# Layer 0's attention one chunk earlier, its router logits as extra columns of the key and value products, and the attention output as the opening term of the experts' sum

## The reference, cut to what matters

```python
xn = layernorm(x)
# attention: 16 heads of 8, linear attention with rope
q, k, v = split(xn @ W_qkv);  q, k = rope(q), rope(k)
qf, kf = elu(q * 8**-0.5) + 1, elu(k) + 1
out = (qf @ (kf.T @ v)) / max(qf @ kf.sum(0), 1e-6)     # per sequence and head
att = out @ W_out
# feed-forward: 64 experts of width 64, top 8 of 4 of 8 groups, and one shared expert
scores = sigmoid(xn @ router_w.T)                        # the logits are 64 columns a token
coef   = 2.5 * normalised top-8 scores (bias added for the choice only)
moe    = sum_e coef[:, e] * ((silu(xn @ Wg[e]) * (xn @ Wu[e])) @ Wd[e])
shared = (silu(xn @ SWg) * (xn @ SWu)) @ SWd
x = x + att + moe + shared
```

## Time and profile before

| | us |
|---|---|
| median of 3 executions | 1829.75 (1829.34 to 1831.74) |
| profiled execution, its own time | 1833.56 |
| its span in the trace | 1831.3 |
| PE busy | 1736.6 (95%) |
| DVE busy | 1348.7 (74%) |
| ACT busy | 803.2 (44%) |
| POOL busy | 609.8 (33%) |
| longest idle of PE in its own rows, chunks 1 to 14 | 0.4 |

### The profile page before, as it was taken

How to read it: one execution, slowest core, us unless ns; L and a number is a source line. 1 busy time by engine, 2 the same in 40 slices (tenths; PEclk the granted TensorE clock), 3 DMA queues, 4 the chain that set the end, 5 groups by cost and what they waited for, 6 DMA issues and landing times.

```text
span 1831.3 us, 25191 instructions
## 1 busy us (share of the span) xinstructions
PE 1736.6 (95%) x7292; PEld 1225.3 (67%) x7292; DVE 1348.7 (74%) x4012; ACT 803.2 (44%) x1439; POOL 609.8 (33%) x637
## 2 busy tenths in 40 slices
PE   3999999999999999999999999999999989888885
PEld 2667777777777777777767677777777766565653
DVE  5667878787878787878787878787878864553447
ACT  4435353535353535353535353535353434432321
POOL 6212142423232323232323232323231333565550
PEclk9999999999999999999999999999999999999988
DMA  7948464636464636463636363636454444666559
GB/s 213 257 125 238 97 157 101 157 95 163 97 161 97 160 97 160 97 161 94 161 96 163 90 167 94 160 95 162 101 148 102 111 143 141 187 204 213 173 158 298
DMA packets 166470, 269.80 MB, mean 147 GB/s; under 512 B 13688, under 2 KB 52344, under 8 KB 166080
## 3 DMA queue, kind: packets, MB, share of 16 engines
q1 hardware_dynamic: 157760, 250.50, 51.9%
q0 software_dynamic: 8576, 17.70, 3.0%
HBM read 202.21 MB, written 65.93 MB: 146 GB/s over the span
## 4 chain that ended last, share of the span: by engine, by line
PE 88%; another core or an unknown queue 3%; issue 3%; ACT 2%; DMA 2%; DVE 2%; POOL 1%; SPq 0%; ACTq 0%; DVEq 0%; POOLq 0%
PE ps_y L656 24%; PE ps_gate L603 8%; PE ps_gate L602 8%; PE ps_gate L601 7%; PE ps_up L601 7%; PE ps_up L603 7%; PE ps_up L602 7%; PE ps_y L682 3%; PE ps_side L622 2%; PE ps_side L601 2%; PE ps_side L603 2%; PE ps_side L602 2%; PE ps_side L791 1%; PE ps_side L774 1%
## 5 line engine op out<-in xcount | busy, mean ns | idle before, releaser
L854 DVE TENSOR_TENSOR silu_h<-ps_up,silu_h 128x512 f32<-128x512 f32 x618 | 424.4, 687 | 401.9 <-ACT silu_h L1260 260.5
L1260 ACT ACTIVATE silu_h<-ps_gate 128x512 f32<-128x512 f32 x618 | 368.0, 599 | 614.1 <-PE ps_gate L603 535.6
L656 PE MATMUL ps_y<-silu_h,w_dn 128*128 128x512 f32 x1056 | 540.6, 593 | 0.4 <-ACT yT L1266 0.4
L848 DVE TENSOR_TENSOR silu_h<-coef_b,silu_h 128x512 f32<-128x512 f32 x528 | 373.9, 708 | 9.0 <-DMA coef_b<-coef_kept 6.6
L601 PE MATMUL ps_gate<-xnT,w_gu 128*128 128x512 f32 x528 | 318.4, 603 | 0.0
L656 PEld LDWEIGHTS ps_y<-silu_h,w_dn 128*128 128x128 f32 x1056 | 199.4, 189 | 55.0 <-issue 7.7
L601 PE MATMUL ps_up<-xnT,w_gu 128*128 128x512 f32 x528 | 210.3, 398 | 11.0 <-DVE silu_h L854 6.6
L602 PE MATMUL ps_gate<-xnT,w_gu 128*128 128x512 f32 x528 | 211.2, 400 | 0.0
L602 PE MATMUL ps_up<-xnT,w_gu 128*128 128x512 f32 x528 | 209.7, 397 | 0.0
L603 PE MATMUL ps_up<-xnT,w_gu 128*128 128x512 f32 x528 | 209.1, 396 | 0.0
L603 PE MATMUL ps_gate<-xnT,w_gu 128*128 128x512 f32 x528 | 207.4, 393 | 0.0
(11 more groups left out here) (265 smaller groups left out, 2719.9 us busy)
## 6 DMA issues: line engine op xcount, KB each, us to landing
coef_b<-coef_kept SPq DMA_DIRECT2D x256, 512.0 KB
slots_x<-empty SPq DMA_DIRECT2D x15, 2080.0 KB, 12.3
w_block<-w_kept SPq DMA_DIRECT2D x45, 512.0 KB
xs<-slots_x SPq DMA_DIRECT2D x37, 260.0 KB
y_back<-y_kept SPq DMA_DIRECT2D x15, 512.0 KB, 7.1
w_raw<-in_ffn_w SPq DMA_DIRECT2D x49, 128.0 KB, 4.1
w_down<-in_ffn_w SPq DMA_DIRECT2D x45, 128.0 KB
xres<-in_x SPq DMA_DIRECT2D x16, 256.0 KB, 3.1
```

The source lines that it names most:

```text
L656: eng.matmul(ps_y[:, :], w_dn[:, j], silu_h[:, g % HBUFS], start=j == 0, stop=last).then_inc(pe_down)
L848: eng.tensor_tensor(silu_h[:, s], coef_b[:, q % COEF_RING, k], silu_h[:, s], ALU.mult).then_inc(dve_h)
L854: eng.tensor_tensor(silu_h[:, s], ps_up[g % 2][:, :], silu_h[:, s], ALU.mult).then_inc(dve_h1)
L1260: eng.activation(silu_h[:, s], ps_gate[g % 2][:, :], ACT.Silu).then_inc(act_silu)
```

## The change

`ATTENTION0` moves to other tiles (6 to 29) and is run for chunk c + 1 in chunk c, after `ROUTE0` in the list; chunk 15 has none of it. In chunk 0 its own attention runs as before (`EARLY0`), and that of chunk 1 by a table of its own (`SECOND0`). `logit0` is gone from chunk 2 on: the router's weights lie beside the value weights, `kv0` to `kv3` are 320 columns wide, ACT copies 192 instead of 128 columns to `v0`, and `score_exp`, now at tile 11, reads the logits there. The product with `w_out` opens the sum in `ps_y` at tile 0 (in chunk 0 it comes at tile 15). The sends of `ROUTE1` are due at tiles 4 to 12 instead of 10 to 21; its `softmax` is at 19 instead of 23, `gate_exp` at 15 instead of 12; `ATTENTION1` is mostly one tile later. `feat_exp` is at 15, `k_feat` 17, `kvsum` 19, `kvmask` 20, `num0` 21.

```diff
-ATTENTION0 = [(0, "kv0"), (1, "kv1"), (2, "kv2"), (3, "kv3"), (4, "k_rope"), (5, "q"), (6, "q_cos"), (6, "q_swap"), (7, "q_sin"), (8, "q_min"),
-              (12, "feat_exp"), (13, "q_feat"), (14, "k_feat"), (16, "kvsum"), (17, "kvmask"), (19, "num0"), (20, "num1"), (20, "mix0"),
-              (24, "mix1"), (26, "mixT")]
+ATTENTION0 = [(6, "kv0"), (7, "kv1"), (8, "kv2"), (9, "kv3"), (10, "k_rope"), (11, "q"), (12, "q_cos"), (12, "q_swap"), (14, "q_sin"), (14, "q_min"),
+              (15, "feat_exp"), (16, "q_feat"), (17, "k_feat"), (19, "kvsum"), (20, "kvmask"), (21, "num0"), (22, "num1"), (23, "mix0"),
+              (24, "mix1"), (29, "mixT")]
...
-ROUTE0 = [(0, "stats0"), (2, "norm0"), (4, "xT0"), (5, "x_lo0"), (8, "logit0"), (10, "score_exp"), (12, "sigmoid0"), (14, "sigmoid1"),
+ROUTE0 = [(0, "stats0"), (2, "norm0"), (4, "xT0"), (5, "x_lo0"), (11, "score_exp"), (13, "sigmoid0"), (15, "sigmoid1"),
           (18, "choice"), (18, "pair4"), (19, "pair2"), (20, "pair1"), (21, "gtop"), (22, "gstrike"), (23, "groups"), (24, "top8"),
           (25, "strike"), (26, "weigh"), (28, "coefT")]
-ROUTE1 = [(5, "stats1"), (7, "norm1"), (8, "xT1"), (9, "x_lo1"), (10, "vl0"), (10, "vl1"), (11, "top1"), (12, "gate_exp"), (23, "softmax"), (30, "select"),
-          (31, "prefix"), (39, "rank"), (40, "key"), (41, "first2"), (42, "slot"), (43, "send0"), (45, "send1"), (47, "send2"), (48, "send3"),
-          (49, "send4"), (51, "send5"), (53, "send6"), (54, "send7")]
+ROUTE1 = [(5, "stats1"), (7, "norm1"), (8, "xT1"), (9, "x_lo1"), (10, "vl0"), (10, "vl1"), (11, "top1"), (15, "gate_exp"), (19, "softmax"), (30, "select"),
+          (31, "prefix"), (33, "rank"), (34, "key"), (35, "first2"), (36, "slot"), (37, "send0"), (38, "send1"), (39, "send2"), (40, "send3"),
+          (42, "send4"), (43, "send5"), (44, "send6"), (45, "send7")]
...
-ATTENTION1 = [(10, "q1"), (11, "v1"), (12, "s0"), (13, "s0_mask"), (13, "s1"), (14, "s1_mask"), (15, "top"), (16, "strike0"), (17, "strike1"),
-              (18, "attend_exp"), (21, "sum0"), (22, "sum1"), (23, "p0"), (23, "near"), (24, "p1"), (24, "self"), (25, "add1"), (26, "hear1"), (26, "mixa"),
...
+ATTENTION1 = [(10, "q1"), (11, "v1"), (13, "s0"), (14, "s0_mask"), (14, "s1"), (15, "s1_mask"), (16, "top"), (17, "strike0"), (18, "strike1"),
+              (19, "attend_exp"), (22, "sum0"), (23, "sum1"), (24, "p0"), (24, "near"), (25, "p1"), (25, "self"), (26, "add1"), (27, "hear1"), (27, "mixa"),
...
-        steps += [(ATTENTION0 if c > 0 else EARLY0, c)]
-        steps += [(ROUTE0, c + 1)] if c + 1 < CHUNKS else []
+        if c == 0:
+            steps += [(EARLY0, 0), (SECOND0, 1), (ROUTE0_SECOND, 1)]
+        elif c + 1 < CHUNKS:
+            steps += [(ROUTE0, c + 1), (ATTENTION0, c + 1)]
...
-                if last:
+                if j == 0 and c > 0:
+                    eng.wait_ge(act_y, c)
+                if j == (0 if c > 0 else FIRST_MIX):
                     eng.wait_ge(*read("mixT", c))
                     eng.wait_ge(w_out_in, 16)
-                    eng.matmul(ps_y[:, :], w_out[:, :], mix_a[:, :], start=False, stop=False).then_inc(pe_mix)
+                    eng.matmul(ps_y[:, :], w_out[:, :], mix_a[:, :], start=j == 0, stop=False).then_inc(pe_mix)
...
-                    mm3(ps[:, 0:2 * P], row(halves(key), int(what[2])), w0_part(2 * P, 4 * P)).then_inc(signal)
+                    mm3(ps[:, 0:2 * P + EXPERTS0], row(halves(key), int(what[2])), w0_part(2 * P, 4 * P + EXPERTS0)).then_inc(signal)
...
+                        for r in range(ROWS):
+                            eng.wait_ge(*read(f"kv{r}", c))
+                        eng.activation(score0[:, :].rearrange("p (r e) -> p r e", r=ROWS), v0[:, :, 0:EXPERTS0], ACT.Exp, scale=-1.0).then_inc(act_score)
...
-                    eng.copy(v0[:, r, 0:P], side_bank(what, c)[:, P:2 * P]).then_inc(read(what, c)[0])
+                    eng.copy(v0[:, r, 0:EXPERTS0 + P], side_bank(what, c)[:, P:2 * P + EXPERTS0]).then_inc(read(what, c)[0])
```

More of the change, by code:

```diff
@@ L85 @@
                 (30, "gates"), (33, "gatesT")]
-ATTENTION1 = [(10, "q1"), (11, "v1"), (12, "s0"), (13, "s0_mask"), (13, "s1"), (14, "s1_mask"), (15, "top"), (16, "strike0"), (17, "strike1"),
-              (18, "attend_exp"), (21, "sum0"), (22, "sum1"), (23, "p0"), (23, "near"), (24, "p1"), (24, "self"), (25, "add1"), (26, "hear1"), (26, "mixa"),
-              (26, "add2"), (27, "hear2"), (27, "mixa_add"), (27, "add3"), (28, "hear3"), (28, "add4"), (29, "hear4"), (32, "mixl"), (32, "mixl_add")]
-ATTENTION1_UNITS = [(at if what == "v1" else at + 2, what) for at, what in ATTENTION1]
+ATTENTION1 = [(10, "q1"), (11, "v1"), (13, "s0"), (14, "s0_mask"), (14, "s1"), (15, "s1_mask"), (16, "top"), (17, "strike0"), (18, "strike1"),
+              (19, "attend_exp"), (22, "sum0"), (23, "sum1"), (24, "p0"), (24, "near"), (25, "p1"), (25, "self"), (26, "add1"), (27, "hear1"), (27, "mixa"),
+              (27, "add2"), (28, "hear2"), (28, "mixa_add"), (28, "add3"), (29, "hear3"), (29, "add4"), (30, "hear4"), (32, "mixl"), (32, "mixl_add")]
+ATTENTION1_UNITS = [(at if what == "v1" else at + (2 if what == "q1" else 1), what) for at, what in ATTENTION1]
 PREP1 = [(28, "w1"), (29, "fold"), (30, "fold_lo"), (31, "zero")]
@@ L99 @@
 EARLY0 = [(1, "feat_exp"), (3, "q_feat"), (4, "k_feat"), (6, "kvsum"), (7, "kvmask"), (8, "num0"), (9, "num1"), (9, "mix0"), (10, "mix1"), (12, "mixT")]
+SECOND0 = [(13, "kv0"), (14, "kv1"), (15, "kv2"), (16, "kv3"), (17, "k_rope"), (17, "q"), (18, "q_cos"), (20, "q_swap"), (21, "q_sin"), (22, "q_min"),
+           (23, "feat_exp"), (24, "q_feat"), (25, "k_feat"), (26, "kvsum"), (27, "kvmask"), (28, "num0"), (29, "num1"), (29, "mix0"), (30, "mix1"), (31, "mixT")]
+ROUTE0_SECOND = [(8, "logit0")] + [(at - (what == "score_exp"), what) for at, what in ROUTE0]
+FIRST_MIX = 15
 TAKES = {"xT0": "x_lo0", "logit0": "score_exp", "coefT": "coefT", "kv0": "kv0", "kv1": "kv1", "kv2": "kv2", "kv3": "kv3",
@@ L209, in build_program @@
         mix_rows = tmp0
-        v0 = sb("v0", [ROWS, P + 1])
+        v0 = sb("v0", [ROWS, EXPERTS0 + P + 1])
         kv = sb("kv", [SEQS, P + HEADS])
@@ L332, in build_program @@
             sem(n) for n in ("dve_kparts", "pool_krope", "pool_kmin", "pool_qrope", "pool_qmin"))
-        act_kexp, act_qexp, act_qrelu, dve_kfeat, pool_qfeat = (
-            sem(n) for n in ("act_kexp", "act_qexp", "act_qrelu", "dve_kfeat", "pool_qfeat"))
+        act_score, act_kexp, act_qexp, act_qrelu, dve_kfeat, pool_qfeat = (
+            sem(n) for n in ("act_score", "act_kexp", "act_qexp", "act_qrelu", "dve_kfeat", "pool_qfeat"))
         dve_gate, act_gate, dve_sel, dve_slot, dve_gw, dve_gates, pool_mark, pool_before, dve_logit1, dve_strike1, act_attend, dve_sum, act_keys = (
@@ L653, in last_products @@
                     eng.wait_ge(w_dn_in[j // DOWN_PART], 16)
-                if j == 0 and c > 0:
-                    eng.wait_ge(act_y, c)
-                eng.matmul(ps_y[:, :], w_dn[:, j], silu_h[:, g % HBUFS], start=j == 0, stop=last).then_inc(pe_down)
+                eng.matmul(ps_y[:, :], w_dn[:, j], silu_h[:, g % HBUFS], start=g == 0, stop=last).then_inc(pe_down)
             def first_of_unit(u):
@@ L700, in step @@
                     for r in range(ROWS):
-                        ins = mm3(ps[:, r * EXPERTS0:(r + 1) * EXPERTS0], row(halves(key), r), w0_part(4 * P, 4 * P + EXPERTS0))
+                        ins = mm3(ps[:, r * EXPERTS0:(r + 1) * EXPERTS0], row(halves(key), r), w0_part(3 * P, 3 * P + EXPERTS0))
                     ins.then_inc(signal)
@@ L724, in step @@
                         for r in (2 * s, 2 * s + 1):
-                            ins = eng.matmul(ps[:, s * (P + 1):(s + 1) * (P + 1)], kf[:, r * P:(r + 1) * P], v0[:, r],
+                            ins = eng.matmul(ps[:, s * (P + 1):(s + 1) * (P + 1)], kf[:, r * P:(r + 1) * P], v0[:, r, EXPERTS0:],
                                              start=r == 2 * s, stop=r == 2 * s + 1)
@@ L883, in step @@
                 elif what == "sigmoid0":
-                    eng.wait_ge(*read("logit0", c))
+                    if c <= 1:
+                        eng.wait_ge(*read("logit0", c))
+                    else:
+                        eng.wait_ge(act_score, c - 1)
                     keep(eng.tensor_scalar(score0[:, :], score0[:, :], 1.0, None, ALU.add))
@@ L1235, in vector @@
             eng.memset(gsel[:, :, :], 0.0)
-            eng.memset(v0[:, :, P:], 1.0).then_inc(dve_const)
+            eng.memset(v0[:, :, EXPERTS0 + P:], 1.0).then_inc(dve_const)
             for n, (what, key) in enumerate(prologue):
@@ L1321, in step @@
                 elif what == "score_exp":
-                    eng.wait_ge(*done("logit0", c))
                     if c > 0:
                         eng.wait_ge(coef_rows, c)
-                    eng.activation(score0[:, :], side_bank("logit0", c)[:, 0:ROWS * EXPERTS0], ACT.Exp, scale=-1.0).then_inc(read("logit0", c)[0])
+                    if c <= 1:
```

(8 more changed lines are left out.)

## The result

The changed kernel takes **1859.68 us** (median of 4, 1858.87 to 1860.74); the kernel before, run beside it, 1830.74 (4 runs). The ratio on record for the runs is 1.0145, interval 1.0127 to 1.0163; the two medians alone give 1.0158, inside it. The kernel is slower, by far more than the 0.2% that a measurement of this kernel can tell. The forecast was 1852, with a range of 1808 to 1862. The profiled execution took 1860.74 for a span of 1858.5, which is 27.2 over the span before.

What follows compares the result with a forecast made beforehand. The prediction took TensorE's (PE's) own queue to bound the steady chunks. From a median of 1829.75: -13.6 PE's work, -7 chunk 15, +32 `num0` waits, +11.5 clock give 1852.7, forecast 1852, range 1808 to 1862.

Steps and rivals of the forecast that it cites:

- likeliest case: PE waits at `num0` for a late `kvmask` in chunks 1 to 14, half followed by clock falls: 1852, chance 0.5.
- the last rival: In chunk 15 DVE's `first2` still waits because a send is late elsewhere: 7 more than the forecast, 1859; chance 0.03.
- PE's work: Logit products removed less 64 added columns: net 1.00 for each of chunks 2 to 15, less 0.34 for chunk 1: -13.6.
- `num0` waits: In chunks 1 to 14 PE waits 2.3 at `num0`, tile 21, for DVE's `kvmask`: +32.
- clock: Half of the 14 waits at `num0` are followed by a lower PE clock, 1.65 each: +11.5.
- chunk 15: DVE's first wait for sends goes; 2 of the 9.2 excess stays for DVE's long tile 20: -7.
- Step 1: From D14, the start of PE's down product in tile 14, DVE and POOL finish `q_min` at D14 + 5.25.
- Step 2: ACT's second exponential then delays DVE, which starts tile 16's product at D16 + 2.75, 2.5 late.
- Step 3: DVE gets no respite: tile 16 takes 2.24, tile 17 2.09 plus 0.60; tile 18's product starts at D16 + 7.68.
- Step 4: From `strike1`'s end to DVE's product after `attend_exp` 3.55, all ACT's; the sum through `kvmask` is D16 + 15.31.
- Step 5: PE reaches `num0` 0.86 into tile 21, at D16 + 13.06, and waits 2.25, with a semaphore's delay 2.3.
- what would show it: Trace signs: L733 idle some 30 us, released by DVE's L995; steady chunk 93.1 or 94.7; 64-column group down to 24 products.

Runs made afterwards that it cites:

- mix_first_separate: `mix_first` with `kv0` to `kv3` back at 256 columns and `logit0` as its own products at tile 8, `score_exp` at 10: 1828.55, ratio 0.9962.
- mix_first: `num_both_22` with layer 0's attention ahead of the routing in each tile and `attend_exp` at tile 20: 1813.57, ratio 0.9889 to the kernel before.
- num_both_22: The changed kernel with `num0` and `num1` both at tile 22, `mix0` left at 23: 1829.46, ratio 0.9982 to the kernel before.
- attend_later: The changed kernel with `attend_exp` at tile 20 instead of 19: 1792.23 on the first chip, ratio 1.0007 to the kernel before.
- before_sends_early: The kernel before with only `rank` to `send7` moved early, at 33 to 45 instead of 39 to 54: 1825.22, ratio 0.9975.
- changed_again: The changed kernel, unedited, run again on the second chip: 1855.25, ratio 1.0123 to the kernel before.

## Why the prediction was right, point by point

It held: slower, by the mechanism of its likeliest case, 7.7 above the forecast and inside the range, if near its upper end. The time alone would not have decided it, since the last rival gave 1859: that one is ruled out by the trace, where `first2` (L1093) waits for nothing in chunk 15. Term by term, on the spans of the two profiles (4.7 of PE's work, 91.0 less 86.3, went from chunk 15 to chunk 0 and counts in neither term):

| term | forecast | measured | from |
|---|---|---|---|
| PE's work | -13.6 | -11.5 | `mix_first_separate` less `mix_first`: 13 x 0.83 + 0.72 |
| `num0` waits | +32 | +29.5 | 93.07 - 91.79 + 0.83 = 2.11, 14 times |
| clock | +11.5 | +12.8 | 94.67 - 93.07 = 1.60, 8 times |
| chunk 15 | -7 | -6.1 | idle 6.24 and 3 for the clock before, 3.15 idle after |
| beyond these, chunks 0, 1, 6 and 7 | 0 | +5.3 | spans of the chunks |
| start and layer 1's experts | 0 | -2.9 | spans |
| sum | +22.9 | +27.1 | spans: +27.2 |

- **PE's work.** The step from one logit product to the next, 0.112, held. A 320-column product, bounded between 0.115 and 0.144, took the upper end, since three of them cost 0.43 (PE's records in tiles 6 to 9). Net 0.83, not 1.00: what was mis-sized is the twelve as a group. Their tile is 1.17 longer with them than without them, in this pair of kernels and between before and after alike, not 1.34. The 0.17 between them is more than one product's step, so not every step of a group is added time; which part the tile spends anyway is not shown.
- **The rule weighed there.** The Trainium skill, page "TensorE: Matmul & The Clock Gate", section "Back-to-back issue gap", gives the price by columns, by which the logits would have been worth no more than the columns added. It gives it for a single product in isolation, and says of that formula that it counts too little for small products in a stream, where the weight load has its share; the prediction left this out. `mix_first_separate` against `mix_first` decides against the price by columns for products of 64.
- **The chain, step by step,** in chunk 8. Step 1: D14 + 4.90 (838.11), forecast 5.25. Step 2: DVE's product of tile 16 at D16 + 2.44, forecast 2.75. Step 3: tiles 16 and 17 took 2.34 and 2.53, forecast 2.24 and 2.69; tile 18's product at D16 + 7.31, forecast 7.68. Step 4: from the end of `strike1` to the product behind `attend_exp` 3.56, forecast 3.55; `kvmask` done at about D16 + 15.0, forecast 15.31. Step 5: PE there at D16 + 13.09, forecast 13.06. Most of the error is step 1's 0.35: POOL's two passes ended 4.02 after `q_sin` began, not 4.38. Four experiments touched the chain: `pair1` out of it, `pair1` twice in it, ACT's link out of it, and `num0` past it; each moved the wait as the steps say, though the last only exchanged it for another.
- **The clock.** "Half of the waits" was a choice from two rows, and that it hit, with 8 of 14, is in good part luck. The runs fill in the rest: behind the waits of 1.14 and 1.33 there was none in 28, behind those of 1.9 to 2.2 there were 8 in 14, twice, behind those of 2.7 and 2.8 nearly always one (27 of 28). But length does not decide alone: the wait of 1.78 in `num_both_22` was followed by a fall, and that of 3.00 in chunk 15 of the changed kernel was not. The Trainium skill, the same page, section "HAM oscillation — how this bites in real kernels", warns only of longer gaps than any of these; in this kernel the shorter ones brought the lower level too, so its figure is no safe bound. Nor is it told by their length which of the 14 fall: the longest, 2.22 in chunk 7, was followed by none in either run, and at the same 1.90 the two runs differ in chunks 2 to 5.
- **Chunk 15.** `first2`'s wait went, as said. What stayed is 3.15 (3.00 of it one wait), not 2: DVE's long tile lasted the 6 forecast (5.86, from 1504.82 to 1510.68), but it began late, since ACT's `attend_exp` at tile 19, with its two table loads, stands just ahead of it, which the forecast left out:

```profile
1504.82 0.69 DVE L862 TENSOR_TENSOR silu_h<-ps_up,silu_h 128x512 f32<-128x512 f32 x1 [2.23 <-ACT silu_h L1271]
...
1510.68 0.68 DVE L862 TENSOR_TENSOR silu_h<-ps_up,silu_h 128x512 f32<-128x512 f32 x1
```

  With `attend_exp` moved, `attend_later` and `mix_first` wait 0.7. `before_sends_early` shows the sends alone to be worth 4.95, of the 7 forecast.
- **Chunks 0 and 1,** costed at nothing, were not: `SECOND0` in chunk 0 makes `kvsum` wait for DVE's `k_feat` (0.8, until 113.05), and chunk 1's first tiles wait 1.65 for DVE's product. The first up product waits 5.6 instead of 4.7, and the clock is low for 6.8 there instead of 3.4; but this is not the change's doing for certain, since in the second trace of the same kernel (`changed_again`) they are 4.2 and 3.4. "PE's work of moved steps is the same in both places" was right; that they meet other waits there was left out.
- **What the other half of "what would show it" said:** 93.1 and 94.7 for the steady chunk came out to 0.1; L733, now L741, has 27.3 of idle time in place of some 30, though put down to "issue" and not to DVE's L995; the group of 64 columns has 24 products.

## What to carry to other kernels

Where one engine is full and all queues are in order, moving a chain of steps earlier or later is worth what its last link meets on the receiving queue, not what it removes: here 0.83 a chunk was gained and 2.1 to 3.7 lost at one semaphore, and three settings of the schedule (`num0` a tile later, the order of the steps within a tile, `attend_exp` a tile later) turned that into a gain of 1.1%. Count a wait on TensorE at its length, some 0.2 us on top, and the clock: the waits of 1.1 and 1.3 us never cost the clock here, those of 1.9 did in half of the cases, those of 2.7 and 2.8 nearly always, at 1.6 us a fall. And when a wait is moved, look at who holds the buffers until then: the second place was worse than the first.

## What was not expected of the hardware

- **One chip differed from the others, in one part of the program alone.** On the first chip the kernel before took 1791.16, on the others 1831 and 1836. The kernel before has no trace from there; those of the four variants that ran there place the 40 us: layer 1's experts take 273 to 276 us, against 311 to 322 elsewhere, while their tiles of layer 0 last as long as on the other chips. On the slower chips ACT pauses there, and so, less often, does DVE; PE is idle for 29 to 36 us of that stretch, against 5 to 7 on the first chip. ACT's waits of `mix_first` have this row, and none of the four traces from the first chip has such a one:

```profile
ACT silu_h L1271 <- remote: 64.3, 12, 6.9
```

  What it waits for is in no row.
- **Falls alternate.** In the changed kernel the clock fell in nearly every other chunk (at 195.8, 383.5, 571.2; then 666.8, 854.5, 1042.3, 1230.0, 1417.7), the distances being two chunks, 187.7; the same wait, in the same place of every chunk, was followed by a fall or not in turn. Why is not shown.
- **An idle record understates the wait.** 0.47 in the records cost 0.9 in the tiles around it, and the 1.90 at `num0` 2.11; at 1.14, 1.33 and 2.78 the chunks show the same 0.2 on top.
